# Rotary cross-attention values by Strassen's seven products, key weights loaded and split in every step

## The chip, the cores and the metric

The kernel runs on one NeuronCore of a Trainium2 chip. The metric is the device time of one execution in microseconds (us). Below, PE is the matrix engine, PEld its weight loads, DVE the vector engine, ACT the scalar engine, POOL the GpSimd engine and SP the queue that issues transfers.

## The reference

A two-layer Perceiver block works on 2 x 128 latent tokens of width 512 against a context of 2 x 2048 rows of width 512: cross-attention with rotary keys, self-attention, a sign-weight layer, a second cross-attention, a second self-attention, a mixture of experts. The change lies in the first of these alone:

```python
lat = layer_norm(latents, ln_lat_g, ln_lat_b)
ctx = layer_norm(context, ln_ctx_g, ln_ctx_b)     # 2 x 2048 x 512
q = lat @ Wq                                      # 16 heads of 64
k, v = jnp.split(ctx @ Wkv, 2, axis=-1)           # 1024 columns each
k = apply_rope(k, cos, sin)
attn = softmax(clip(q k^T * scale, -11, 11))
out = (attn @ v) @ Wo + bo
```

The products `ctx @ Wkv` (4096 x 512 x 2048) are made in three passes, high times high, high times low, low times high, with each operand split into a rounded part and a rest, so that the rounded form of the matmul keeps its accuracy.

## The kernel before

The context goes through `cross_attention_rotary` in `NC` = 8 blocks `n` of 512 rows, and each block in four steps `t` = 4n to 4n+3, one for each group of four heads: 32 steps in all. I call 4n, 4n+1, 4n+2, 4n+3 the first to fourth step of block n. Every engine runs a stream of its own, written out by hand, in order; semaphores join them. There is no scheduler.

- PE: in the first and third step `values(v)` makes half of the value columns of the block: four tiles of 128 rows x 512 columns, each 4 depths x 3 passes = 12 matmuls of 512 columns, 48 in a call and 96 in a block, into the four banks of `u_ps`. Behind it `transposes` turns two of the four depths of block n+1 into `u_ps`. Then in each step `project(t)` (24 matmuls into the two banks of `k_ps`), `scores(t-1)` (into all of `u_ps`) and `weigh(t-2)` (into `o_ps`).
- ACT: copies the values out of `u_ps` (`values`), writes the scaled context twice, as it is and rounded (`context`, into `ctx_full` and `ctx_hi`), takes exponents (`exponent`), and takes the square root for the layer norm two blocks ahead (`root`) in the third step.
- DVE: `turn(t)` rotates the keys, four multiplies out of `k_ps` and two of SBUF alone; `clip(t-1)`; and the layer norm of block n+2 in three pieces in the second, third and fourth step (`stats`, `spread`, `center`).
- POOL: `split` makes the context's low part from `ctx_full` and `ctx_hi`, two depths in every other step; `add_up(t-1)` adds the probabilities into the denominators, four instructions a step.
- SP: all weights are loaded and split once. `load_ctx` and `load_tab` have two buffers each.

The split of the weights is done before step 0, or at step 1 for two of the four key groups (`high_v`, `low_v`, `high_k`, `low_k`). PE's order in a step reads, cut:

```python
if t < NT and t % 2 == 0:
    values(v)
    ...
if t < NT:
    project(t)
if 1 <= t <= NT:
    scores(t - 1)
if t >= 2:
    weigh(t - 2)
```

## Time and profile before

| | us |
|---|---|
| median of three runs | 1193.29 (1192.87 to 1197.12) |
| the profiled execution | 1196.15 |
| its span, first to last instruction | 1194.4 |
| PE busy in it | 1174.4 |
| DVE, ACT, POOL busy | 688.8, 540.1, 217.0 |
| the stage of the change | about 0 to 542 of the span |

Times are of one execution on the slowest core. In a timeline a row is a run of equal instructions: start, time until the last of them ends, and how many. Matmul ends are modelled and overlap the next start, so a matmul's price is the distance between starts.

### The profile page before, as it was taken

How to read it: one execution, taken by the hardware profiler on the slowest of the kernel's cores; microseconds unless marked ns; L12 is line 12 of the kernel's file. 1: busy time of each engine (PE TensorE's matmuls, PEld its weight loads, DVE VectorE, ACT ScalarE, POOL GpSimd, SP SyncE). 2: the span in 40 equal slices, each digit the busy share in tenths (PEclk: the TensorE clock that was granted, in tenths of full speed). 3: DMA queues.
4: the chain of work that ended last, by engine and by line, in shares of the span. 5: the costliest groups of instructions: out<-in, count | busy, mean ns of one | idle time of the engine just before them, and what ended most of it. 6: DMA issues, size and time to landing. Idle time of an engine off the chain costs nothing.

```text
span 1194.4 us, 23415 instructions
## 1 busy us (share of the span) xinstructions
PE 1174.4 (98%) x9888; PEld 963.8 (81%) x9888; DVE 688.8 (58%) x1220; ACT 540.1 (45%) x907; POOL 217.0 (18%) x178
## 2 busy tenths in 40 slices
PE   8999999999999999999899999999999999999998
PEld 6888888888788888864546667888899999999997
DVE  4654554545464533466788885265765566566562
ACT  4433324332433322224359997373644544444441
POOL 2243343444333443350000000010000000000000
PEclk9999999999999999999989999999999999999999
DMA  8210201010100020245232324301545445445440
GB/s 302 71 55 1 66 2 52 4 36 19 36 19 2 27 72 1 83 139 212 96 152 79 136 108 178 142 1 72 228 159 211 161 192 211 157 195 207 158 162 19
DMA packets 28160, 126.06 MB, mean 106 GB/s; under 512 B 2715, under 2 KB 2971, under 8 KB 17572
## 3 DMA queue, kind: packets, MB, share of 16 engines
q1 hardware_dynamic: 28068, 124.74, 27.9%
q8 instruction: 69, 1.13, 0.4%
q14 instruction: 23, 0.19, 0.0%
HBM read 124.20 MB, written 0.52 MB: 104 GB/s over the span
## 4 chain that ended last, share of the span: by engine, by line
PE 49%; issue 2%; DVE 2%; ACT 2%; DVEq 0%
PE mid_bk L57 11%; PE mid_bk L58 10%; PE mid_bk L59 10%; PE mid_bk L1105 5%; PE mid_bk L1120 2%; PE mid_bk L1150 2%; PE mid_bk L1076 2%; PE mid_bk L995 2%; PE mid_bk L1140 1%; PE mid_bk L1249 0%; ACT sa_sc L1415 0%; PE mid_bk L1201 0%; PE mid_bk L1190 0%; PE mid_bk L1050 0%; PE mid_bk L986 0%
## 5 line engine op out<-in xcount | busy, mean ns | idle before, releaser
L565 POOL TENSOR_TENSOR norm_both<-norm_both,prob 128x512 f32<-128x512 f32 x118 | 155.4, 1317 | 145.6 <-DVE prob L357 138.2
L494 ACT ACTIVATE prob<-u_ps 128x512 f32<-128x512 f32 x128 | 66.2, 605 | 181.5 <-PE u_ps L667 181.5
L57 PE MATMUL mid_bk<-mo_x_hi,mo_w_hi 128*128 128x256 f32 x496 | 141.0, 284 | 0.0
L58 PE MATMUL mid_bk<-mo_x_lo,mo_w_hi 128*128 128x256 f32 x496 | 141.0, 284 | 0.0
L59 PE MATMUL mid_bk<-mo_x_hi,mo_w_lo 128*128 128x256 f32 x496 | 141.0, 284 | 0.0
L340 DVE TENSOR_TENSOR turned<-k_ps,tabs 128x512 f32<-128x512 f32 x32 | 22.1, 690 | 189.7 <-PE k_ps L59 189.6
L1788 DVE TENSOR_TENSOR mo_w_lo<-w_raw,mo_w_hi 128x2048 fp32r<-128x2048 f32 x32 | 73.3, 2292 | 72.7 <-ACT mo_w_hi L1497 72.7
L57 PE MATMUL k_ps<-ctx_hi,wk_hi 128*128 128x512 f32 x256 | 102.8, 402 | 0.0
L57 PE MATMUL u_ps<-wv_hi,ctx_hi 128*128 128x512 f32 x256 | 101.7, 397 | 0.8 <-ACT prob L494 0.8
L483 ACT ACTIVATE vals<-u_ps 128x512 f32<-128x512 f32 x64 | 38.3, 598 | 141.2 <-PE u_ps L59 141.1
L1497 ACT ACTIVATE mo_w_hi<-w_raw 128x2048 fp32r<-128x2048 f32 x32 | 61.2, 1913 | 87.9 <-PE mid_bk L59 87.9
L57 PE MATMUL mid_bk<-mo_w_hi,mo_h_hi 128*128 128x512 f32 x256 | 100.2, 391 | 0.0
L58 PE MATMUL k_ps<-ctx_lo,wk_hi 128*128 128x512 f32 x256 | 100.2, 391 | 0.0
L58 PE MATMUL u_ps<-wv_lo,ctx_hi 128*128 128x512 f32 x256 | 100.1, 391 | 0.0
L58 PE MATMUL mid_bk<-mo_w_lo,mo_h_hi 128*128 128x512 f32 x256 | 100.0, 391 | 0.0
L59 PE MATMUL u_ps<-wv_hi,ctx_lo 128*128 128x512 f32 x256 | 99.7, 389 | 0.0
L59 PE MATMUL k_ps<-ctx_hi,wk_lo 128*128 128x512 f32 x256 | 99.7, 389 | 0.0
L59 PE MATMUL mid_bk<-mo_w_hi,mo_h_lo 128*128 128x512 f32 x256 | 99.6, 389 | 0.0
L58 PEld LDWEIGHTS mid_bk<-mo_x_lo,mo_w_hi 128*128 128x128 f32 x496 | 95.9, 193 | 1.2
L57 PEld LDWEIGHTS mid_bk<-mo_x_hi,mo_w_hi 128*128 128x128 f32 x496 | 95.8, 193 | 1.2
L59 PEld LDWEIGHTS mid_bk<-mo_x_hi,mo_w_lo 128*128 128x128 f32 x496 | 95.8, 193 | 0.0
L1505 ACT ACTIVATE mo_hid<-mid_bk,mo_b_cur 128x256 f32<-128x256 f32 x128 | 53.7, 472 | 86.8 <-PE mid_bk L59 86.7
(264 smaller groups left out, 2357.2 us busy)
## 6 DMA issues: line engine op xcount, KB each, us to landing
w_raw<-in_w SPq DMA_DIRECT2D x64, 1024.0 KB, 6.3
ctx_raw<-in_ctx_rows SPq DMA_DIRECT2D x8, 1024.0 KB, 5.5
x_k<-in_ctx_T SPq DMA_DIRECT2D x8, 1024.0 KB, 7.0
x_val<-in_ctx_heads SPq DMA_DIRECT2D x8, 1024.0 KB, 5.0
tabs<-in_rot_tabs SPq DMA_DIRECT2D x8, 512.0 KB, 3.8
vals<-in_wq_rows SPq DMA_DIRECT2D x4, 512.0 KB, 7.6
ctx_raw<-in_wo SPq DMA_DIRECT2D x1, 2048.0 KB, 9.7
x_mask<-in_mask SPq DMA_DIRECT2D x2, 1024.0 KB, 9.0
```

The costliest lines, as they stand in the source:

```text
L57: pe.matmul(out, w_hi, x_hi, start=start, stop=False)
L58: pe.matmul(out, w_hi, x_lo, start=False, stop=False)
L59: return pe.matmul(out, w_lo, x_hi, start=False, stop=stop)
L483: act.activation(vals[:, i, hv * 512:(hv + 1) * 512], u_ps[:, i, :], ACT.Copy).then_inc(s["v_out"], 1)
L494: act.activation(prob[:, t % 2, i, :], u_ps[:, i, :], ACT.Exp).then_inc(s["exped"], 1)
L565: ins = pool.tensor_tensor(to, to, src, ALU.add)
L995: ins = pe.matmul(bk[b][:, m, :], normed_T[:, k, b * P:(b + 1) * P], (wq, wk, wv)[m][:, k, :], start=(m == 2 and k == 0), stop=(k == KD - 1))
L1076: pe.matmul(s_ps[:, a, :], normed_T[rows, g, b * P:(b + 1) * P], k_raw[rows, n % 2, c * 512:(c + 1) * 512], start=True, stop=True).then_in ...
L1105: ins = pe.transpose(turned_at(q, a)[:, k * P:(k + 1) * P], x_sc[:, n % 2, a, (4 * c + k) * P:(4 * c + k + 1) * P], ident[:])
L1497: act.activation(w2_hi[:, r, :, :], w2_raw[:, r, :, :], ACT.Copy).then_inc(mo["w2_hi"], 1)
L1505: act.activation(hid[:, r, n, :], h_ps[:, 2 * r + n // 2, (n % 2) * TOK:(n % 2 + 1) * TOK], ACT.Gelu_apprx_tanh, bias=b1_cur[:, r, n:n + 1 ...
L1788: dve.tensor_tensor(w2_lo[:, r, :, :], w2_raw[:, r, :, :], w2_hi[:, r, :, :], ALU.subtract).then_inc(mo["w2_lo"], 1)
```

## The change

Each block's values are a product of a 512 x 512 context block A with the 512 x 1024 weights B. A is cut into row halves and depth halves, B into depth halves and column halves; the product of the 2 x 2 blocks is made with seven products of half depth instead of eight, by the Winograd form of Strassen's scheme. Four sums of context blocks (S1 to S4) and four of weight blocks (T1 to T4) are needed, and each sum needs its own high and low part. For a row quarter pair `ip` (0 or 1) `values(n, ip)` makes seven `product`s of 2 depths x 3 passes = 6 matmuls of 512 columns, 42 a call, 84 a block. Three of them accumulate on a bank that already holds another product.

What is new, by engine:

- PE: `values(n, 0)` stands at the end of the second step, `values(n, 1)` between the two halves of `project` in the third. All four `transposes` of block n+1 stand at the head of the fourth step.
- DVE: `weight_sums` and seven `low_v` at the start; in every step `low_k(t+1)` ahead of the rotation; `sums(n)` in the first step (four half-tile sums in place in `ctx_full`), then `stats` and `spread` for block n+1 in that same step; `low_s(n)` in the second; `add_products` (five adds out of `u_ps`) at the end of the second and inside the third; `center` of block n+1 at the head of the third.
- ACT: `high_k(t+1)` in every step; `high_s(n)` and `root(n+1)` at the end of the first step; `keep_products` (two copies); `context` for all four depths at the head of the fourth.
- POOL: `split` for all four depths in the fourth step, ahead of `add_up`.
- SP: key weights (512 KB) are loaded in every step once the step before the last is projected; `ctx_raw` and `tabs` have one buffer each; the output weights are loaded behind the last value product.

Core of the diff:

```diff
+        a_of = {"A11": (0, 0, 0), "A12": (0, 1, 0), "A22": (0, 1, 1),
+                "S2": (1, 0, 0), "S4": (1, 1, 0), "S3": (1, 0, 1), "S1": (1, 1, 1)}
+        w_of = {"B11": 0, "B21": 1, "B22": 2, "T3": 3, "T1": 4, "T2": 5, "T4": 6}
...
             def load_tab(n):
-                if n >= 2:
-                    sp.wait_ge(s["rope"], 24 * (n - 1))
+                if n >= 1:
+                    sp.wait_ge(s["rope"], 24 * n)
...
+            def load_wk(t):
+                g = t % 4
+                if t >= 2:
+                    sp.wait_ge(s["k_mm"], 2 * (t - 1))
+                sp.dma_start(wk_raw[:, t % 2, :, :], I["wk_rows"][g * P:(g + 1) * P, :]
+                             .rearrange("p (k n) -> p k n", k=KD)).then_inc(s_wk[t % 2], 16)
...
+            for t in range(1, NT):
+                n, r = t // 4, t % 4
+                if t + 1 < NT:
+                    load_wk(t + 1)
+                if r == 0:
+                    load_tab(n)
+                if r == 3 and n + 2 < NC:
+                    load_ctx(n + 2)
...
+            def weight_sums():
+                dve.wait_ge(s["wv_in"], 64)
+                for n, (dst, a, b) in enumerate((("T1", "T3", "B11"), ("T2", "B22", "T1"), ("T3", "B22", "T3"),
+                                                 ("T4", "B21", "T2"))):
+                    dst, a, b = (wv_raw[:, w_of[m], :, :] for m in (dst, a, b))
+                    if n:
+                        dve.wait_ge(s["part_sum"], n)
+                    dve.tensor_tensor(dst, a, b, ALU.subtract).then_inc(s["part_sum"], 1)
+
+            def low_v(j):
+                dve.wait_ge(s["part_hi"], j + 1)
+                dve.tensor_tensor(wv_lo[:, j, :, :], wv_raw[:, j, :, :], wv_hi[:, j, :, :],
+                                  ALU.subtract).then_inc(s["part_lo"], 1)
...
+            def low_k(t):
+                dve.wait_ge(s["wk_hi"], t + 1)
+                dve.tensor_tensor(wk_lo[:, t % 2, :, :], wk_raw[:, t % 2, :, :], wk_hi[:, t % 2, :, :],
+                                  ALU.subtract).then_inc(s["wk_lo"], 1)
...
+            def sums(n):
+
+                dve.wait_ge(s["csplit"], 4 * n + 4)
+                for m, (dst, a, b, op) in enumerate((("A22", "A21", "A22", ALU.add), ("A21", "A11", "A21", ALU.subtract),
+                                                     ("A11", "A22", "A11", ALU.subtract),
+                                                     ("A12", "A12", "A11", ALU.subtract))):
+                    if m:
+                        dve.wait_ge(s["part_sum"], 4 + 4 * n + m)
+                    dve.tensor_tensor(full[dst], full[a], full[b], op).then_inc(s["part_sum"], 1)
+
+            def low_s(n):
+                for u in range(2):
+                    dve.wait_ge(s["part_hi"], NWB + 2 * n + u + 1)
+                    ks = slice(2 * u, 2 * u + 2)
+                    dve.tensor_tensor(s_lo[:, ks, :], ctx_full[:, ks, :], s_hi[:, ks, :],
+                                      ALU.subtract).then_inc(s["part_lo"], 1)
+
+            def add_products(n, ip):
+
+                v = 2 * n + ip
+                c11, c12 = vals[:, ip, 0:512], vals[:, ip, 512:1024]
+                c21, c22 = vals[:, 2 + ip, 0:512], vals[:, 2 + ip, 512:1024]
+                dve.wait_ge(s["v_kept"], 2 * v + 1)
+                dve.wait_ge(s["v_mm"], NWB * v + 2)
+                dve.tensor_tensor(c12, u_ps[:, 1, :], c11, ALU.add).then_inc(s["v_sum"], 1)
+                dve.wait_ge(s["v_mm"], NWB * v + 3)
+                dve.wait_ge(s["v_sum"], 5 * v + 1)
+                dve.tensor_tensor(c22, u_ps[:, 2, :], c12, ALU.add).then_inc(s["v_sum"], 1)
+                dve.wait_ge(s["v_mm"], NWB * v + 4)
+                dve.wait_ge(s["v_sum"], 5 * v + 2)
+                dve.tensor_tensor(c22, u_ps[:, 3, :], c22, ALU.add).then_inc(s["v_sum"], 1)
+                dve.wait_ge(s["v_mm"], NWB * v + 6)
+                dve.tensor_tensor(c21, u_ps[:, 2, :], c12, ALU.add).then_inc(s["v_sum"], 1)
+                dve.wait_ge(s["v_mm"], NWB * v + 7)
+                dve.tensor_tensor(c12, u_ps[:, 3, :], c12, ALU.add).then_inc(s["v_sum"], 1)
+
...
             for t in range(NT + 1):
-                n, g = t // 4, t % 4
+                n, r = t // 4, t % 4
+                if t < NT and r == 2 and n + 1 < NC:
+                    center(dve, n + 1)
+                if t + 1 < NT:
+                    low_k(t + 1)
                 if t < NT:
-                    turn(t)
+                    if r == 1:
+                        low_s(n)
+                    turn_first(t)
+                    if r == 2:
+                        add_products(n, 1)
+                    turn_second(t)
+                    if t == 0:
+                        for j in range(3, NWB):
+                            low_v(j)
+                    if r == 0:
+                        sums(n)
                 if t >= 1:
                     clip(t - 1)
-                if t == 1:
-                    low_k(2)
-                    low_k(3)
-                if t < NT and 2 <= n + 2 < NC:
-                    if g == 1:
-                        stats(dve, n + 2)
-                    elif g == 2:
-                        spread(dve, n + 2)
-                    elif g == 3:
-                        center(dve, n + 2)
-                if t == 28:
+                if t < NT:
+                    if r == 1:
+                        add_products(n, 0)
+                    if r == 0 and n + 1 < NC:
+                        stats(dve, n + 1)
+                        spread(dve, n + 1)
+                if t == 11:
                     dve.wait_ge(s["bo_in"], 16)
...
+            def high_k(t):
+                act.wait_ge(s_wk[t % 2], 16 * (t // 2 + 1))
+                if t >= 2:
+                    act.wait_ge(s["k_mm"], 2 * (t - 1))
+                act.activation(wk_hi[:, t % 2, :, :], wk_raw[:, t % 2, :, :], ACT.Copy).then_inc(s["wk_hi"], 1)
+
+            def high_s(n):
+                act.wait_ge(s["part_sum"], 4 + 4 * n + 4)
+                for u in range(2):
+                    ks = slice(2 * u, 2 * u + 2)
+                    act.activation(s_hi[:, ks, :], ctx_full[:, ks, :], ACT.Copy).then_inc(s["part_hi"], 1)
...
+            def keep_products(n, ip):
+
+                v = 2 * n + ip
+                c11 = vals[:, ip, 0:512]
+                act.wait_ge(s["v_mm"], NWB * v + 1)
+                if n >= 1:
+                    act.wait_ge(s["weighed"], 4 * n)
+                act.activation(c11, u_ps[:, 0, :], ACT.Copy).then_inc(s["v_kept"], 1)
+                act.wait_ge(s["v_sum"], 5 * v + 1)
+                act.wait_ge(s["v_mm"], NWB * v + 5)
+                act.activation(c11, u_ps[:, 0, :], ACT.Copy).then_inc(s["v_kept"], 1)
...
+                n, r = t // 4, t % 4
+                if t < NT and r == 3 and n + 1 < NC:
+                    for k in range(KD):
+                        context(n + 1, k, k)
+                if t + 1 < NT:
+                    high_k(t + 1)
+                if t == 0:
+                    for j in range(3, NWB):
+                        high_v(j)
...
+                if t < NT and r == 2:
+                    keep_products(n, 1)
                 if t >= 1:
                     exponent(t - 1)
-                if t < NT and n + 2 < NC and g == 2:
-                    root(act, n + 2)
+                if t < NT and r == 0:
+                    high_s(n)
+                    if n + 1 < NC:
+                        root(act, n + 1)
+                if t < NT and r == 1:
+                    keep_products(n, 0)
...
-                if t < NT and t % 2 == 0 and n + 1 < NC:
-                    for kk in range(2):
-                        split(n + 1, 2 * (t % 4 // 2) + kk)
+                if t < NT and t % 4 == 3 and n + 1 < NC:
+                    for k in range(KD):
+                        split(n + 1, k)
...
+            def values(n, ip):
+
+                v = 2 * n + ip
+                if n == 0 and ip == 0:
+                    pe.wait_ge(s["part_lo"], NWB)
+                if ip == 1:
+                    pe.wait_ge(s["v_sum"], 5 * v)
+                    pe.wait_ge(s["v_kept"], 2 * v)
+                for bank, (a, w) in enumerate((("A11", "B11"), ("S2", "T2"), ("S3", "T3"), ("S1", "T1"))):
+                    if ip == 0:
+                        pe.wait_ge(s["exped"], 16 * n + bank + 1)
+                    if bank == 1:
+                        pe.wait_ge(s["part_lo"], NWB + 2 * n + 2)
+                    if v == 9 and bank >= 2:
+                        pe.wait_ge(s["den_out"], bank - 1)
+                    product(n, ip, a, w, bank, True, True)
+                pe.wait_ge(s["v_kept"], 2 * v + 1)
+                product(n, ip, "A12", "B21", 0, False, True)
+                pe.wait_ge(s["v_sum"], 5 * v + 2)
+                product(n, ip, "A22", "T4", 2, False, True)
+                pe.wait_ge(s["v_sum"], 5 * v + 3)
+                product(n, ip, "S4", "B22", 3, False, True)
+
...
-                if t < NT and t % 2 == 0:
-                    v = t // 2
-                    if v == 0:
-                        pe.wait_ge(s["cfull"], KD)
-                    values(v)
-                    if v // 2 + 1 < NC:
-                        for kk in range(2):
-                            pe.wait_ge(s["v_out"], 4 * v + kk + 1)
-                            transposes(v // 2 + 1, 2 * (v % 2) + kk, kk)
+                n, r = t // 4, t % 4
+                if t < NT:
+                    if r == 3 and n + 1 < NC:
+                        for k in range(KD):
+                            transposes(n + 1, k, k)
+                    project(t, 0)
...
-                if t < NT:
-                    project(t)
-                if 1 <= t <= NT:
+                    if r == 2:
+                        values(n, 1)
+                    project(t, 1)
+                if t >= 1:
                     scores(t - 1)
                 if t >= 2:
                     weigh(t - 2)
+                if t < NT and r == 1:
+                    values(n, 0)
...
```

DVE around the first step of a block. In the kernel before, the stretch from the clip of a first step's probabilities on; `prob` holds probabilities, `cst` the layer norm's statistics, `turned` and `part` the rotated keys:

```order
L357 TENSOR_SCALAR prob<-prob 128x512 x4
L296 BN_STATS cst<-ctx_raw 128x6 x4
L340 TENSOR_TENSOR turned<-k_ps,tabs 128x512
L341 TENSOR_TENSOR turned<-k_ps,tabs 128x512
L345 TENSOR_TENSOR part<-k_ps,tabs 128x512
L346 TENSOR_TENSOR part<-k_ps,tabs 128x512
```

Behind a clip and the statistics the next rotation follows at once. In the changed kernel, from `sums` of a block's first step to the rotation of its second:

```order
L349 TENSOR_TENSOR ctx_full<-ctx_full 128x2x256 x4
L407 TENSOR_SCALAR prob<-prob 128x512 x4
L299 BN_STATS cst<-ctx_raw 128x6 x4
L304 BN_AGGR cmv<-cst 128x2 x4
L306 TENSOR_SCALAR cva<-cmv 128x4
L338 TENSOR_TENSOR wk_lo<-wk_raw,wk_hi 128x1024
L355 TENSOR_TENSOR s_lo<-ctx_full,s_hi 128x1024 x2
L386 TENSOR_TENSOR turned<-k_ps,tabs 128x512
L387 TENSOR_TENSOR turned<-k_ps,tabs 128x512
L395 TENSOR_TENSOR part<-k_ps,tabs 128x512
L396 TENSOR_TENSOR part<-k_ps,tabs 128x512
```

The context sums, the whole of the statistics, the key split and the sums' low parts now stand between one rotation and the next.

ACT at the same place, with the semaphores that each waits for. Before, the root stands behind exponents in the third step:

```order
L315 ACT_TABLE_LOAD
L315 ACTIVATE csd<-cva 128x4 [waits x0_c_var]
L494 ACT_TABLE_LOAD [waits x0_summed,x0_weighed]
L494 ACTIVATE prob<-u_ps 128x512 [waits x0_score]
L494 ACTIVATE prob<-u_ps 128x512 [waits x0_summed,x0_weighed,x0_score] x3
L483 ACTIVATE vals<-u_ps 128x512 [waits x0_weighed,x0_v_mm] x4
```

Changed:

```order
L519 ACTIVATE s_hi<-ctx_full 128x1024 [waits x0_part_sum]
L519 ACTIVATE s_hi<-ctx_full 128x1024
L318 ACT_TABLE_LOAD
L318 ACTIVATE csd<-cva 128x4 [waits x0_c_var]
L513 ACTIVATE wk_hi<-wk_raw 128x1024 [waits x0_k_mm,x0_wk_in0]
L557 ACT_TABLE_LOAD [waits x0_summed,x0_weighed]
L557 ACTIVATE prob<-u_ps 128x512 [waits x0_score]
L557 ACTIVATE prob<-u_ps 128x512 [waits x0_summed,x0_weighed,x0_score] x3
L546 ACTIVATE vals<-u_ps 128x512 [waits x0_weighed,x0_v_mm]
```

The rounded key weights of the next step (`wk_hi`) now stand behind the root, and the root behind DVE's `cva`.

POOL in a fourth step, changed (`ctx_lo` is the context's low part, `norm_both` the denominators):

```order
L631 TENSOR_TENSOR norm_both<-norm_both,prob 128x512 [waits x0_summed,x0_clipped]
L631 TENSOR_TENSOR norm_both<-norm_both,prob 128x512 [waits x0_summed] x3
L617 TENSOR_TENSOR ctx_lo<-ctx_full,ctx_hi 128x512 [waits x0_cfull] x4
L631 TENSOR_TENSOR norm_both<-norm_both,prob 128x512 [waits x0_summed,x0_clipped]
L631 TENSOR_TENSOR norm_both<-norm_both,prob 128x512 [waits x0_summed] x3
```

Before, two of the four `ctx_lo` rows stood there and two two steps earlier.

## Rows read from the trace of the kernel before

**Rows 1.** The page: busy time of each engine, granted clock in 40 slices

```profile
PE 1174.4 (98%) x9888; PEld 963.8 (81%) x9888; DVE 688.8 (58%) x1220; ACT 540.1 (45%) x907; POOL 217.0 (18%) x178
...
PEclk9999999999999999999989999999999999999999
```

**Rows 2.** Waits of PE, span 60 to 520 us, then 0 to 60

```profile
PE u_ps L667 <- ACT prob L494: 0.3, 1, 0.3
...
PE u_ps L57 <- ACT prob L494: 0.8, 1, 0.8
```

**Rows 3.** Timeline of PE, one step with values: start us, us, engine line op

```profile
114.94 0.50 PE L57 MATMUL u_ps<-wv_hi,ctx_hi 128*128 128x512 f32 x1
...
126.00 1.03 PE L602 MATMUL u_ps<-ident,ctx_raw 128*128 128x128 f32 x8
126.79 0.48 PE L57 MATMUL k_ps<-ctx_hi,wk_hi 128*128 128x512 f32 x1
...
132.42 2.07 PE L667 MATMUL u_ps<-q_T,turned 32*128 32x128 f32 x64
134.41 1.97 PE L683 MATMUL o_ps<-prob,vals 128*64 128x128 f32 x32
```

**Rows 4.** Timeline of DVE, steps around the same place

```profile
115.57 2.46 DVE L296 BATCH_NORM_STATS2 cst<-ctx_raw 128x6 f32<-128x512 f32 x4
...
132.53 0.69 DVE L345 TENSOR_TENSOR part<-k_ps,tabs 128x512 f32<-128x512 f32 x1 [1.36 <-PE k_ps L59]
...
134.33 0.68 DVE L351 TENSOR_TENSOR turned<-turned,part 128x512 f32<-128x512 f32 x1
135.13 1.90 DVE L357 TENSOR_SCALAR prob<-prob 128x512 f32<-128x512 f32 x4
136.94 0.37 DVE L301 BATCH_NORM_AGGREGATE cmv<-cst 128x2 f32<-128x6 f32 x4
137.35 1.08 DVE L303 TENSOR_SCALAR cva<-cmv 128x4 f32<-128x4 f32 x1
```

**Rows 5.** Timeline of ACT, the same steps

```profile
126.69 0.78 ACT L468 ACTIVATE ctx_full<-u_ps,vecs 128x512 f32<-128x512 f32 x1
127.35 0.78 ACT L468 ACTIVATE ctx_hi<-u_ps,vecs 128x512 fp32r<-128x512 f32 x1
...
134.50 2.07 ACT L494 ACTIVATE prob<-u_ps 128x512 f32<-128x512 f32 x4 [5.03 <-PE u_ps L667]
...
138.46 0.21 ACT L315 ACTIVATE csd<-cva 128x4 f32<-128x4 f32 x1 [0.59 <-DVE cva L303]
138.68 1.28 ACT L494 ACT_TABLE_LOAD   x1
```

**Rows 6.** Timeline of POOL, the same steps

```profile
128.21 2.63 POOL L551 TENSOR_TENSOR ctx_lo<-ctx_full,ctx_hi 128x512 fp32r<-128x512 f32 x2 [7.06 <-ACT ctx_hi L468]
137.11 5.40 POOL L565 TENSOR_TENSOR norm_both<-norm_both,prob 128x512 f32<-128x512 f32 x4 [6.26 <-DVE prob L357]
```

**Rows 7.** DVE and POOL at once: two timelines, and DVE's line 409 (min/median/max ns)

```profile
146.75 5.84 DVE L310 TENSOR_SCALAR ctx_raw<-ctx_raw,cmv,crs 128x512 f32<-128x512 f32 x4
...
L409 DVE TENSOR_TENSOR resid<-resid,bo x2: 684/1235/1786, 478.9 to 479.5; 128x512 f32<-128x512 f32 x2
...
479.02 6.09 POOL L565 TENSOR_TENSOR norm_both<-norm_both,prob 128x512 f32<-128x512 f32 x4 [15.07 <-DVE prob L357]
```

**Rows 8.** Timeline of the start, all engines

```profile
17.12 10.53 PE L614 MATMUL k_ps<-norm_both,vals 128*128 128x256 f32 x48
...
22.11 2.01 ACT L451 ACTIVATE wv_hi<-prob 128x1024 fp32r<-128x1024 f32 x2
...
27.30 0.58 PE L57 MATMUL u_ps<-wv_hi,ctx_hi 128*128 128x512 f32 x1
...
27.68 0.60 ACT L474 ACTIVATE q_T<-k_ps 128x512 f32<-128x512 f32 x1 [2.85 <-PE k_ps L614]
...
29.79 1.23 DVE L328 TENSOR_TENSOR wk_lo<-prob,wk_hi 128x1024 fp32r<-128x1024 f32 x1 [1.22 <-ACT wk_hi L456]
```

**Rows 9.** Transfers: KB each, median us from issue to landing

```profile
tabs<-in_rot_tabs SPq DMA_DIRECT2D x8, 512.0 KB, 3.8
```

**Rows 10.** Stretches behind a gap of PE: busy of each engine, granted clock

```profile
580.00:582.00 2.00, 0.66 (x4) 0.42 (x4) 1.89 (x7) 1.47 (x4) 0.00 (x0) 1.00 0.00 0
...
584.00:586.00 2.00, 2.00 (x23) 1.38 (x16) 0.93 (x2) 0.00 (x0) 0.00 (x0) 0.50 0.00 0
```

More of the change, by code:

```diff
@@ L185, in cross_attention_rotary @@
-        slabs = sb_in(st, "slabs", [P, 64 * 256 + (env["floor"] - env["base"]) // 4])
+        NWB = 7
+        wv_raw = place("wv_raw", [P, NWB, 2, 512], 0)
+        wv_lo, wv_hi = (place(n, [P, NWB, 2, 512], kb, F32R) for n, kb in (("wv_lo", 0), ("wv_hi", 28)))
+        wk_raw = place("wk_raw", [P, 2, KD, 256], 56)
+        wk_lo, wk_hi = (place(n, [P, 2, KD, 256], kb, F32R) for n, kb in (("wk_lo", 56), ("wk_hi", 64)))
+        ctx_full = place("ctx_full", [P, KD, 512], 72)
+        s_lo, s_hi = (place(n, [P, KD, 512], kb, F32R) for n, kb in (("s_lo", 72), ("s_hi", 80)))
@@ L633, in project, with product @@
[L633 to L646 removed]
+            def product(n, ip, a, w, bank, start, stop):
+                src, kh, th = a_of[a]
+                rows = slice(256 * th + ip * P, 256 * th + ip * P + P)
+                for kk in range(2):
+                    k = 2 * kh + kk
+                    hi, lo = ((ctx_hi[:, n % 2, k, rows], ctx_lo[:, n % 2, k, rows]),
+                              (s_hi[:, k, rows], s_lo[:, k, rows]))[src]
+                    for part_a, part_b in ((hi, wv_hi), (hi, wv_lo), (lo, wv_hi)):
+                        ins = pe.matmul(u_ps[:, bank, :], part_a, part_b[:, w_of[w], kk, :],
+                                        start=(start and kk == 0 and part_a is hi and part_b is wv_hi),
+                                        stop=(stop and kk == 1 and part_a is lo), skip_group_check=True)
+                ins.then_inc(s["v_mm"], 1)
```

270 lines of the change are left out of this document (102 added, 168 removed).

## The prediction

> **What bounds the kernel now.** I read the page first: PE is busy for 1174.4 of 1194.4 us, at full clock nearly throughout, and no other engine above 58% [rows 1]. Busy PE is not PE at its peak, so I went to PE's waits: between 60 and 520 us it waits 0.3 us in all, before that 0.8 us once for an exponent [rows 2]. The stage of the change is therefore PE's own time, and each matmul taken out there is worth its distance between starts, as long as nobody else gets late. DVE, at half load on average, is the engine to watch: the change gives it work in a fixed order, and PE's new waits hang on the end of that order.
>
> **What is removed.** The 48 matmuls of a value call take from 114.94 to 126.00 [rows 3]: 0.230 us each. A call of 42 takes 9.7 us. Eight blocks with 12 fewer each: 96 x 0.230 = **22.1 us less**. Everything else that PE does stays: `project` 5.7 (126.79 to 132.42), `scores` 2.0, `weigh` 1.9, eight transposes 0.8 [rows 3].
>
> **What is added, and its prices.** Per block DVE gets four key splits and two sum splits of 1024 columns (1.2 each, as the 1.23 of wk_lo [rows 8]), four context sums and ten product adds (0.68 each alone, 0.60 in a queue [rows 4]), some 17 us in all. ACT gets four key copies and two sum copies of 1.0 (2.01 for two [rows 8]) for eight copies of values less. On average that fits. Whether it hides is a question of order, at three places.
>
> *1. From the rotation of the first step to the value products of the second, every block.* Zero is the start of `scores` in the first step (132.42 in the trace). PE then has scores 2.0, weigh 1.9, project 5.7, scores 2.0, weigh 1.9, values 9.7: it would be through at 23.2. But the last two products wait for `add_products`, and DVE reaches it only after: end of the rotation, 2.6 (rows 132.42 to 134.33 + 0.68 [rows 3, 4]); four sums that each wait for the one before, 2.8; clip 1.8 and statistics 2.5, aggregate and cva 0.4 + 1.1 [rows 4]; then, over on ACT, the root 0.3 and the key copy 1.0, which stands behind it [rows 5, 8]; back on DVE the key split 1.2, the sum splits 2.4, six rotation instructions 3.6, clip 1.8, two product adds 1.4; and on PE the last two products, 2.8. Sum: 25.7. PE ends **2.5 us late**, part of it ahead of the first product (the exponents stand on ACT behind the same root, key copy and a 1.28 table load [rows 5]), part ahead of the sixth.
>
> *2. The first projection of a new block.* It waits for all four `split` on POOL, now queued behind `add_up`. Zero is the end of scores in the third step. POOL starts on add_up at 2.7 (exponents 2.1, last clip 0.5), needs 5.4 for it and 5.3 for the splits (2.63 for two) [rows 4 to 6]: 13.4. PE has weigh 1.9, transposes 1.6, project 5.7, scores 2.0, weigh 1.9: 13.1. Late by **0.3**. ACT is in time: its eight context writes at 0.66 [rows 5] end at 8.0, the key copy at 9.1.
>
> *3. DVE and POOL at once.* Line 409, an add of two SBUF tiles, takes 0.684 us alone and 1.786 with an add_up begun beside it, and that add_up takes 6.09 in place of 5.40; four scalings of the clips' kind and size, which take 1.90 for four alone [rows 4], take 5.84 beside an add_up [rows 6, 7]. So one waits for the other's running instruction. The multiplies out of `k_ps` show no such rows. The Trainium skill, "SBUF — State Buffer", section "Who interferes with whom", calls this pair of ports an exclusive lock for a whole instruction, for DVE instructions with two SBUF inputs and those that use both ports. That speaks against this change: by it the sum is the forecast's, by a collision only where one has been seen it would be the first rival's. The change adds just such instructions. In the fourth step the key split (1.1) and one of the two SBUF adds of the rotation (0.6) fall between the four splits: these end 1.8 later, the stall of place 2 is 0.3 + 1.8 = **2.1**, in two blocks 1.4, because there the first instruction of add_up is a short copy. The clip and add_up behind shift too, and the next key split pushes add_up out by 1.2 more, to some 4 us behind the next zero of place 1, so that the rotation's two SBUF adds of the first step wait for it: 1.9 more there, **4.4** in all. In the last block, without statistics and root, the same collisions leave 1.9.
>
> *4. The start.* Before, value products begin at 27.30, with weights split while PE makes the queries [rows 8]. Now the first key copy stands behind the last query copy (27.68 + 0.5), so: key copy to 29.2, key split to 30.4, project 30.5 to 36.2. DVE has four dependent weight sums at 1.25 (to 35.4), three weight splits (38.9), the second key split (40.1), then the first rotation, for which `project(1)` waits: 41.4 to 47.1; scores to 49.2. DVE: rotation ends 43.7, four weight splits 48.4, context sums 51.2, statistics and cva 54.3. ACT: root 54.5, key copy 55.5, table load 56.8, first exponent 57.4. Only now is a bank of `u_ps` free for the values; DVE's key split 56.7, sum splits 59.1, rotation 62.7, clip 64.5, two adds 65.9, and the last products end at 68.7. PE's own work in it is 5.7 + 5.7 + 2.0 + 9.7 = 23.1, from 27.3 to 50.4. Late by 18.3; less the 0.8 that before waits [rows 2]: **17.5**.
>
> Costed at nothing: key loads (512 KB; a table of that size lands in 3.8 [rows 9], from the end of a projection to its next use are 13 us, cover of 5 on top of load, copy and split); the single table buffer (its load starts with the end of the fourth step's rotation and lands about as the next block's second half is projected; late by 1 at most, behind POOL's delay); the single context buffer (loaded a step and a half ahead); the late output weights (20 us of PE lie between). The output bias at step 11 and the reciprocals and scaling at 18 and 19 stand in a fuller DVE queue: 2 in all.
>
> **The sum.** -22.1 + 17.5 + 6 x 4.4 (blocks 1 to 6) + 1.9 + 5 x 2.1 + 2 x 1.4 + 2 = **+39.0 us**. From the profiled execution, 1196.15, that is 1235.2; it lies 2.9 above the median of the runs, so in their terms **1232**.
>
> **The rivals.**
> - *The lock costs little*: POOL's or DVE's collisions fall between instructions. For it: most overlaps in before left no mark on rotation rows. Against: line 409 and the scalings. Then -22.1 + 17.5 + 6 x 2.5 + 7 x 0.3 + 1 = +13.6: **1207**.
> - *The order has room after all* (the other side): if the DVE chain of place 1 is shorter than 23.2 rather than 25.7, for instance because dependent sums and adds follow as closely as independent ones (0.6, some 1 us less) and cva doesn't meet an add_up (0.9 less), and the lock costs nothing, only the start is left: -22.1 + 17.5 = -4.6, **1189**, no change that can be told. It decides from 2.5 us less in the chain. It turns faster only if the start also costs under 16.
> - *The clock falls too.* Behind gaps of PE around 580 us the granted clock went from 1.00 to 0.50, 2.4 to 1.2 GHz [rows 10]; what PE does in 4 us of it takes 2 more. The new gaps are 2 to 3 us at 13 places, and 5 and 8 at the start. Ahead of the sixth product it hides behind DVE; at a block's first projection it moves the next zero but gives POOL the same time. I take 1 each: **1247**. The skill's page "TensorE: Matmul & The Clock Gate", Part 1, says that idleness is what throttles the array; the rows at 580 agree, and by it the range must reach up.
>
> **How the numbers follow.** Forecast 0.55 (its own range 1221 to 1240), lock costs little 0.23, clock or worse 0.12, room after all 0.10. Cutting 0.10 at each end gives 1203 to 1246. This kernel's measurement can't tell less than about 0.5%, 6 us, from no change. Faster 0.04, same 0.07, slower 0.89.
>
> **What would show it.** Right: value matmuls 672 in place of 768; PE waits of 2 us for POOL's `ctx_lo` at each block's first projection; waits ahead of the first and sixth product of each second step for ACT's exponents and DVE's adds; PE idle near 36 to 41 and 49 to 57 us; cva, key split and rotation SBUF adds with long maxima; some 66 us a block where before has 62. Wrong: blocks of 62 with no lock marks (first rival), or 59 (second); waits for `wk_raw` or `tabs` transfers, which I took as hidden; a clock under 1.00 within the blocks.

## The result, and the profile after

The changed kernel takes **1218.92 us** (median of 4 runs, 1216.31 to 1220.99) against 1193.08 for the kernel before on the same chip: ratio **1.0209**, interval 1.0177 to 1.0242. It is 25.8 us slower; I had forecast 39.0 slower (1232, range 1203 to 1246). The profiled execution has a span of 1219.2.

The page answers [rows 1]: PE has 96 matmuls fewer and is busy for 11.7 us less, over a span that is 24.8 longer. PEclk, the granted clock in tenths, shows a 7 in the second slice.

```profile
PE 1162.7 (95%) x9792; PEld 948.5 (78%) x9792; DVE 810.3 (66%) x1383; ACT 566.8 (46%) x922; POOL 230.9 (19%) x178
...
PEclk9799999999999999999989999999999999999999
```

What PE waits for, 14 to 75 us and then 75 to 520 us (us in total, times, longest), where [rows 2] has 0.8 and 0.3:

```profile
PE u_ps L694 <- ACT prob L557: 6.6, 1, 6.6
PE k_ps L57 <- DVE turned L387: 3.4, 1, 3.4
PE k_ps L57 <- DVE wk_lo L338: 2.9, 1, 2.9
...
PE u_ps L694 <- ACT prob L557: 9.0, 6, 2.1
PE k_ps L57 <- issue: 7.5, 7, 1.4
PE u_ps L694 <- DVE vals L368: 3.7, 7, 0.6
PE u_ps L694 <- DVE s_lo L355: 1.0, 1, 1.0
```

By the places of the prediction, the first three are the start (place 4). Of the others, the second line is the first projection of a block (place 2; "issue" because the profile names no releaser), the rest the value products of the second step (place 1).

PE's timeline at the start, and in one block around a first projection, the two `scores` behind it and the value call:

```profile
30.44 0.53 PE L57 MATMUL k_ps<-ctx_hi,wk_hi 128*128 128x512 f32 x1 [2.89 <-DVE wk_lo L338]
...
41.18 0.77 PE L57 MATMUL k_ps<-ctx_hi,wk_hi 128*128 128x512 f32 x1 [3.43 <-DVE turned L387]
...
48.34 2.07 PE L757 MATMUL u_ps<-q_T,turned 32*128 32x128 f32 x64
56.98 0.77 PE L694 MATMUL u_ps<-wv_hi,ctx_hi 128*128 128x512 f32 x1 [6.57 <-ACT prob L557]
...
161.77 0.47 PE L57 MATMUL k_ps<-ctx_hi,wk_hi 128*128 128x512 f32 x1 [1.41 <-issue]
...
167.42 2.07 PE L757 MATMUL u_ps<-q_T,turned 32*128 32x128 f32 x64
...
182.45 0.50 PE L694 MATMUL u_ps<-wv_hi,ctx_hi 128*128 128x512 f32 x1 [1.47 <-ACT prob L557]
...
190.41 0.50 PE L694 MATMUL u_ps<-wv_hi,ctx_hi 128*128 128x512 f32 x1 [0.55 <-DVE vals L368]
```

The same stretch on DVE and POOL, to be held against [rows 4, 6]:

```profile
156.16 1.39 DVE L338 TENSOR_TENSOR wk_lo<-wk_raw,wk_hi 128x1024 fp32r<-128x1024 f32 x1 [6.41 <-ACT wk_hi L513]
...
168.74 1.74 DVE L398 TENSOR_TENSOR turned<-turned,part 128x512 f32<-128x512 f32 x1
170.40 0.68 DVE L401 TENSOR_TENSOR turned<-turned,part 128x512 f32<-128x512 f32 x1
...
178.03 1.27 DVE L306 TENSOR_SCALAR cva<-cmv 128x4 f32<-128x4 f32 x1
180.52 1.23 DVE L338 TENSOR_TENSOR wk_lo<-wk_raw,wk_hi 128x1024 fp32r<-128x1024 f32 x1 [1.22 <-ACT wk_hi L513]
```

```profile
155.16 6.50 POOL L617 TENSOR_TENSOR ctx_lo<-ctx_full,ctx_hi 128x512 fp32r<-128x512 f32 x4
163.63 6.29 POOL L631 TENSOR_TENSOR norm_both<-norm_both,prob 128x512 f32<-128x512 f32 x4 [1.97 <-DVE prob L407]
175.28 5.35 POOL L631 TENSOR_TENSOR norm_both<-norm_both,prob 128x512 f32<-128x512 f32 x4 [5.35 <-DVE prob L407]
```

The reader is to see an overlap in each long row: the rotation's sum at 168.74 takes 1.74, not 0.68, with an `add_up` running to 169.9; `cva`, four columns, takes 1.27 with another running; and the four splits take 6.50, not 5.3, with DVE's key split among them.

**A second number for what follows.** The first matmul of the self-attention behind the changed stage starts at 542.85 before and at 563.93 after. So 21.1 of the profile's 24.8 arise in the changed stage; 3.7 come later, from code that is the same in both. I call the first difference the **stage's**, and give it for each run (one execution each, with its sign against before).

### The profile page after: what moved, and what is told of

Read it like the earlier page. It is cut to its first block, busy times and chain, and to the rows that moved or that the text cites. A ratio compares the mean times of both kernels' runs of the same rounds, so it can differ in the third digit from the quotient of the medians.

```text
span 1219.2 us, 23526 instructions
## 1 busy us (share of the span) xinstructions
PE 1162.7 (95%) x9792; PEld 948.5 (78%) x9792; DVE 810.3 (66%) x1383; ACT 566.8 (46%) x922; POOL 230.9 (19%) x178
## 4 chain that ended last, share of the span: by engine, by line
PE 46%; DVE 3%; issue 2%; ACT 2%; DMA 0%; DVEq 0%; ACTq 0%
PE mid_bk L57 10%; PE mid_bk L58 10%; PE mid_bk L59 10%; PE mid_bk L1198 5%; PE mid_bk L1213 2%; PE mid_bk L1243 2%; PE mid_bk L1169 2%; PE mid_bk L1088 2%; PE mid_bk L1233 1%; DMA w_raw<-in_w 0%; PE mid_bk L1342 0%; DVE mo_w_lo L1875 0%; DVE mo_w_lo L1881 0%; ACT sa_sc L1508 0%; PE mid_bk L1294 0%
## 5 line engine op out<-in xcount | busy, mean ns | idle before, releaser
L631 POOL TENSOR_TENSOR norm_both<-norm_both,prob 128x512 f32<-128x512 f32 x118 | 159.1, 1348 | 208.5 <-DVE prob L407 201.1
L1881 DVE TENSOR_TENSOR mo_w_lo<-w_raw,mo_w_hi 128x2048 fp32r<-128x2048 f32 x32 | 73.3, 2291 | 74.5 <-ACT mo_w_hi L1590 74.5
L338 DVE TENSOR_TENSOR wk_lo<-wk_raw,wk_hi 128x1024 fp32r<-128x1024 f32 x32 | 43.5, 1359 | 63.7 <-ACT wk_hi L513 63.7
L1789 DVE CUSTOM_DVE_ANT_0 x_sc<-mid_bk,x_mask 128x512 f32<-128x512 f32 x128 | 80.9, 687 | 5.6 <-issue 5.6
L1198 PEld LDWEIGHTS mid_bk<-ident,x_sc 128*128 128x128 f32 x512 | 55.3, 140 | 25.8 <-ACT x_pT L1530 18.7
L1875 DVE TENSOR_TENSOR mo_w_lo<-w_raw,mo_w_hi 128x2048 fp32r<-128x2048 f32 x31 | 70.8, 2285 | 4.9 <-ACT mo_w_hi L1582 4.9
L1523 ACT ACTIVATE x_sc<-x_sc,x_negtop 128x1024 f32<-128x1024 f32 x64 | 73.5, 1149 | 1.2 <-DVE x_negtop L1796 1.2
## 6 DMA issues: line engine op xcount, KB each, us to landing
wv_raw<-in_wv_rows SPq DMA_DIRECT2D x4, 512.0 KB, 12.1
```

The lines of the kernel that those rows point to most:

```text
L631: ins = pool.tensor_tensor(to, to, src, ALU.add)
L1198: ins = pe.transpose(turned_at(q, a)[:, k * P:(k + 1) * P], x_sc[:, n % 2, a, (4 * c + k) * P:(4 * c + k + 1) * P], ident[:])
L1523: act.activation(cut, cut, ACT.Exp, bias=x_neg[:, n % 2, a:a + 1], accum_out=x_den[:, n % 2, half, a:a + 1]).then_inc(x["exped"], 1)
L1789: dve.tensor_tensor_reduce(x_sc[:, n % 2, a, cols], s_ps[:, a, :], mask[:, b, cols], 1.0, -3.0e38, ALU.add, ALU.max, x_tops[:, n % 2, a, c ...
L1875: dve.tensor_tensor(w1_lo[:, r, :, :], w1_raw[:, r, :, :], w1_hi[:, r, :, :], ALU.subtract).then_inc(mo["w1_lo"], 1)
L1881: dve.tensor_tensor(w2_lo[:, r, :, :], w2_raw[:, r, :, :], w2_hi[:, r, :, :], ALU.subtract).then_inc(mo["w2_lo"], 1)
```

## The experiments

All are edits of the changed kernel. Medians against the kernel before on the same chip (1192.4 to 1193.4).

| run | median | ratio (interval) | stage's |
|---|---|---|---|
| changed kernel | 1218.9 | 1.0209 (1.0177 to 1.0242) | +21.1 |
| e1_root_behind | 1213.8 | 1.0166 (1.0136 to 1.0195) | +19.1 |
| e2_norm_later | 1216.7 | 1.0192 (1.0169 to 1.0215) | +15.4 |
| e3_splits_first | 1227.9 | 1.0295 (1.0267 to 1.0323) | +31.9 |
| e4_start_early | 1211.1 | 1.0148 (1.0115 to 1.0182) | +15.6 |
| e5_narrow | 1193.1 | 0.9994 (0.9982 to 1.0006) | -2.3 |
| e6_nokeys | 1191.8 | 0.9991 (0.9976 to 1.0005) | -3.0 |
| e7_start_mix | 1203.0 | 1.0074 (1.0047 to 1.0101) | +8.9 |
| e8_five | 1185.5 | 0.9955 (0.9932 to 0.9978) | -8.9 |
| e9_pool_waits | 1235.1 | 1.0337 (1.0309 to 1.0365) | +41.4 |
| e10_five_waits | 1189.4 | 0.9976 (0.9962 to 0.9990) | -5.6 |
| e11_four | 1187.6 | 0.9961 (0.9947 to 0.9975) | -7.9 |
| e12_one_shared | 1189.2 | 0.9971 (0.9952 to 0.9989) | -4.4 |

My theory at the outset: DVE's order and the lock with POOL cost the blocks their gain, and the order of copies and splits costs the start. The rivals: POOL's lateness without the lock, or the key loads.

**e1_root_behind.** ScalarE, first step:

```diff
+                        high_k(t + 2)
                         root(act, n + 1)
```

> ScalarE's copy of the next step's key weights moved ahead of the root in each first step; nothing else. If place 1 is set by VectorE's chain (it waits some 1.2 us for that copy between cva and the key split, and PE stands 2.0 us a block behind the chain): about 1.2 us in each of seven blocks, 8 us less, 1210, and the waits ahead of the second step's value products shrink. Rival, POOL's add_up and the lock set place 1: no change, 1219.

The median is 5.1 lower, but the stage gave only 2.0 of it. The wait of the first product for the exponents fell from 9.0 to 3.0, and one product later PE waited 6.0 for `s_lo`, the low parts of the context sums, instead of 1.0: the sum splits stand behind the key split. A wait removed ahead of an in-order queue moved one instruction on.

**e2_norm_later.** DVE's `stats` and `spread` of the next block, and the root, go from the first step to the third:

```diff
-                    if r == 0 and n + 1 < NC:
+                if t < NT and r == 2 and n + 1 < NC:
                     stats(dve, n + 1)
                     spread(dve, n + 1)
...
+                if then_center:
+                    center(dve, n + 1)
                 dve.wait_ge(s["v_mm"], NWB * v + 6)
```

> Statistics, aggregates, cva and the root of the next block moved out of the first step into the third (centring between the third and the fourth product add). By the theory of the chain it is 3.5 us shorter with the wait for the root and its table gone, against a stall of 2.0 a block: 7 x 2.0 = 14 less, and some 4 less at the start, where the first exponent stands behind the same root: about 1201. Rival, the third step has no room for them (VectorE's moved 5.4 us come back as a wait of the transposes or of the second rotation): 1215 to 1225. Rival, the lock sets place 1: 1215.

The median fell by 2.2, the stage's number by 5.7. The third step had room. But the shorter chain now meets POOL's `add_up`. DVE, and POOL's row beside it:

```profile
173.99 2.14 DVE L338 TENSOR_TENSOR wk_lo<-wk_raw,wk_hi 128x1024 fp32r<-128x1024 f32 x1 [1.68 <-ACT wk_hi L513]
176.05 4.53 DVE L355 TENSOR_TENSOR s_lo<-ctx_full,s_hi 128x1024 fp32r<-128x1024 f32 x2
```

```profile
172.39 7.10 POOL L631 TENSOR_TENSOR norm_both<-norm_both,prob 128x512 f32<-128x512 f32 x4 [5.36 <-DVE prob L409]
```

Key split and sum splits take 6.7 together where the changed kernel's take 3.6: 3.1 of the 3.5 us taken out of the chain went back into the lock.

**e3_splits_first.** POOL:

```diff
+                if t % 4 == 2 and n + 1 < NC:
+                    continue
                 if t < NT and t % 4 == 3 and n + 1 < NC:
                     for k in range(KD):
                         split(n + 1, k)
+                    add_up(t - 2)
```

> POOL makes the four context splits of the next block ahead of the add_up of the second step's probabilities instead of behind it. If PE's wait of 1.4 us at a block's first projection (place 2) is for POOL: 7 x 1.4 = 10 less, 1209. Rival, the two add_ups that now follow the splits reach into the next block and take VectorE's rotation and ScalarE's exponents with them: no change or up to 10 more.

9.0 slower, the rival's case. The wait at place 2 is gone, so it was POOL's; but PE's largest waits of 75 to 520 us became:

```profile
PE u_ps L697 <- ACT prob L557: 20.1, 6, 4.1
PE u_ps L697 <- DVE s_lo L355: 3.1, 1, 3.1
```

All waits of 75 to 520 us grew by only 3.2, from 21.2 to 24.4, while the stage grew by 10.8. The rest is TensorE's clock: in six blocks it is granted at 0.50 for a while, and some 55 matmuls start 0.43 us apart in place of 0.23, about 11 us. One such stretch (us, us, busy and number of PE, PEld, DVE, ACT, POOL, then the granted clock, DMA share, GB/s):

```profile
248.50:255.30 6.80, 5.91 (x14) 4.66 (x15) 6.80 (x12) 2.89 (x6) 0.00 (x0) 0.50 0.00 0
```

**e4_start_early.** On DVE `weight_sums()` first, then both key splits; on ScalarE:

```diff
             queries(1)
+            high_k(0)
+            high_k(1)
             queries(2)
-            queries(3)
-            high_k(0)
             for j in range(3):
                 high_v(j)
+            queries(3)
```

> Order at the start only: weight sums, then both key splits at once on VectorE; both key copies and three value copies between the query copies on ScalarE. If the start is lost to the order of the copies and splits (VectorE is idle from 14 to 29 us), project(0) begins at 28 in place of 30.4, the 3.4 us wait of project(1) goes, and the first value product comes at 50 in place of 57: 7 us less, 1212. Rival, the value weights' transfers land too late for the sums (issued up to 9.6 us, 12 us to land): half of it, 1215. Rival, TensorE's clock stays at its lower level longer, since the gaps move: 1217.

7.8 less, and PE's rows stand where they were expected:

```profile
28.50 0.49 PE L57 MATMUL k_ps<-ctx_hi,wk_hi 128*128 128x512 f32 x1 [1.27 <-DVE wk_lo L338]
...
50.32 0.77 PE L696 MATMUL u_ps<-wv_hi,ctx_hi 128*128 128x512 f32 x1 [8.30 <-ACT prob L558]
```

DVE's weight sums start at 22.22, when the last value weights have landed, instead of 30.30. So the order made this part of place 4. Not all of it: the first value product still waits 8.3 for the exponents.

**e5_narrow.** POOL's tiles cut:

```diff
-                        ins = pool.tensor_tensor(to, to, src, ALU.add)
+                        ins = pool.tensor_tensor(to[:, :, 0:16], to[:, :, 0:16], src[:, :, 0:16], ALU.add)
```

> POOL's add_up adds 16 of 128 columns (all but the first copy of a group): most of the sum of the denominators is left out, and with it nearly all of POOL's 5.4 us a step; PE, ScalarE and VectorE do the same work as in the changed kernel. If POOL delays place 2 (its splits stand behind add_up) and the lock stretches the rotation's sum of place 1: 7 x 1.4 = 10 and 7 x 1.1 = 8 less, 1201. Rival, POOL only delays place 2: 1209. Rival, POOL's time doesn't matter: 1219.

25.8 less, more than even the first theory's 18: the stage gave 23.4. At place 1 nothing but 0.2 a block is left:

```profile
PE u_ps L694 <- DVE vals L368: 1.1, 6, 0.2
```

In its DVE rows the rotation's sum takes 0.68 and `cva` 0.17. From the start of `scores`, the chain to the key split takes 10.9 where the changed kernel's takes 13.1 (167.42 to 180.52): 2.2 less, the two lock marks.

**e6_nokeys.**

```diff
             def low_k(t):
+                if t >= 2:
+                    return
                 dve.wait_ge(s["wk_hi"], t + 1)
```

(likewise the load and the copy.)

> Key weights are loaded and split in the first two steps alone; every later step uses the two pieces that are there (the keys of half of the heads are left out). This takes the key copy, the key split and the wait between them out of the chain of place 1 (2.4 us with 2.0 of stall) and one lock collision out of place 2 (0.1 of the splits' 6.5). By the theory of the chain: 7 x 2.0 = 14 less and 1 to 2 at the start, 1204. Rival, VectorE's place in the queue is made by POOL's lock: 1215. Rival, the loads themselves cost (queue, bandwidth): less than 1200.

27.2 less (stage 24.0), where 15 were expected. I had priced the meeting of key split and context splits at 0.1. POOL's splits show more:

```profile
150.72 5.43 POOL L623 TENSOR_TENSOR ctx_lo<-ctx_full,ctx_hi 128x512 fp32r<-128x512 f32 x4
```

5.43 in place of 6.50, and the wait at place 2 falls from 7.5 to 1.7. So of the 1.41 at a block's first projection 1.0 is one DVE instruction, the key split, locking POOL out. e5 and e6 take away different things and win nearly the same, 23.4 and 24.0: each alone brings DVE and POOL back under PE's time; the loss was an excess over a threshold, not a sum of shares.

**e7_start_mix.** e2 and e4 together, and:

```diff
-                if t < NT and r == 0:
+                if t < NT and r == 0 and n:
                     high_s(n)
+                if t == 1:
+                    high_s(0)
```

> The early start and the later statistics together, and in the first block alone the exponents ahead of the copies of the context sums. If the start is a chain of copies and splits: the first value product comes at 42 us in place of 50 (early start) and 57 (changed kernel), the second one waits until 47 for the split of the context sums, the last ends at 56: 5 to 7 us less than the early start alone, and 2 for the statistics: 1203. Rival, the gap between the first and the second product costs what is gained (and the clock falls there): 1209.

1203.0, as expected; the first product starts at 43.65, the second at 48.58 (42 and 47 forecast). The stage's 12.2 are e2's 5.7, e4's 5.5 and 1.0 that no run separates: the start and the blocks add up.

**e8_five.** e7, and:

```diff
-                if 0 < t < NT - 1:
+                if 0 < t < NT - 1 and r != 1:
                     low_k(t + 1)
...
                     turn_second(t)
+                if r == 1:
+                    low_k(t + 1)
```

with two of the four splits on DVE between its two halves of the rotation in the fourth step.

> e7_start_mix, with the key split of the second step behind the rotation instead of ahead of the split of the context sums, and with two of the four context splits of a block on VectorE. If VectorE's order and POOL's queue hold PE back: 7 x 1.0 (s_lo), 7 x 0.55 (product adds) and 7 x 1.4 (place 2) less than e7_start_mix: 1183, below the kernel before. Rival, the lock between VectorE and POOL turns the shared splits and the sum splits into longer ones (in e2_norm_later the same two took 4.53 instead of 2.35 beside an add_up): 1192 to 1197.

**1185.5**, 17.6 under e7 and 0.45% under the kernel before: the lowest median of all. PE's waits of 75 to 520 us:

```profile
PE u_ps L705 <- DVE vals L368: 4.0, 6, 1.4
PE k_ps L57 <- issue: 0.5, 2, 0.3
PE u_ps L768 <- ACT prob L565: 0.3, 1, 0.3
```

Some 3 us of the 17.8 that the stage gained over e7 are none of the edit's aims. Behind the wait for `s_lo` in the first block, 3.3 in both, the clock fell in the profiled execution of e7 and not in that of e8. The same stretch in e7, then in e8:

```profile
48.00:54.00 6.00, 5.42 (x13) 4.29 (x14) 5.97 (x12) 0.00 (x0) 0.57 (x1) 0.50 0.01 4
```

```profile
48.00:54.00 6.00, 5.69 (x24) 4.42 (x24) 6.00 (x12) 0.00 (x0) 0.00 (x0) 1.00 0.01 3
```

**e9_pool_waits.**

```diff
                 pool.wait_ge(s["clipped"], 4 * t + 4)
+                if g == 3 and t < NT - 1:
+                    pool.wait_ge(s["part_lo"], NWB + 2 * (n + 1) + 2)
```

> The changed kernel, all work kept; POOL's add_up of each fourth step waits until VectorE has made the context sums' splits of the next block. e5_narrow took away POOL's lateness and the lock together; this takes away one meeting of the lock at place 1 alone (cva takes 1.27 in place of 0.17 beside that add_up) and leaves place 2 as it is. If the lock makes the stall of place 1: cva at 0.17, 6 or 7 x 1.1 = 7 to 8 less, 1211. Rival, e5_narrow gained by POOL being free, not by the lock: the stall stays and the later add_up makes others wait, 1219 to 1228.

A miss: 16.2 slower in place of 7 to 8 faster. DVE, from `cva` to the clips, and POOL:

```profile
182.63 0.17 DVE L306 TENSOR_SCALAR cva<-cmv 128x4 f32<-128x4 f32 x1
...
189.83 1.03 DVE L398 TENSOR_TENSOR turned<-turned,part 128x512 f32<-128x512 f32 x1
190.79 1.78 DVE L401 TENSOR_TENSOR turned<-turned,part 128x512 f32<-128x512 f32 x1
192.50 2.51 DVE L407 TENSOR_SCALAR prob<-prob 128x512 f32<-128x512 f32 x4
```

```profile
187.65 6.07 POOL L633 TENSOR_TENSOR norm_both<-norm_both,prob 128x512 f32<-128x512 f32 x4 [13.12 <-issue]
```

The mechanism did what I said: `cva` takes 0.17 with POOL held back. But the same `add_up` now meets the rotation's two sums and the clips behind it (0.35, 1.1 and 1.1 longer than in the changed kernel), closer to the product adds, and the wait ahead of the sixth product grows from 3.7 to 17.7, up to 3.1 each. The waits for exponents fall from 9.0 to 3.8, so all waits of 75 to 520 us grow by 7.8, from 21.2 to 29.0. The stage grew by 20.3. Most of the other 12.5 is the clock: at each of the six long waits it goes to 0.50, and some 55 matmuls start 0.43 apart, about 11 us. The sixth product here, then the same place in the changed kernel:

```profile
196.45:199.20 2.75, 2.75 (x7) 2.17 (x8) 0.69 (x1) 0.73 (x1) 2.59 (x3) 0.50 0.00 0
```

```profile
190.40:193.20 2.80, 2.79 (x12) 2.33 (x13) 1.38 (x2) 1.10 (x2) 2.64 (x3) 1.00 0.00 0
```

Not a wrong mechanism but a wrong price: I had counted what the wait frees, and neither what it moves onto nor the clock behind longer waits.

**e11_four, e10_five_waits, e12_one_shared.** e11 is e8 with all four splits on POOL; e10 is e8 with e9's wait; e12 is e8 with one shared split:

```diff
-                        for k in (2, 3):
+                        for k in (3,):
```

> e8_five without the context splits shared with VectorE: the order of the second step alone beside e7_start_mix. If e8_five's 17.6 under e7_start_mix came from the order (s_lo 7.4, product adds 3.7) and from place 2 (7.5) as the waits say: 1193. Rival, the two are one stall moved about (what one place gives back the other takes): 1203 or 1186.

> e8_five with the wait of e9_pool_waits: the sum splits at 2.35 in place of 3.44 and the rotation's sum at 0.68 in place of 1.77 in the second step. If the 4.0 us of waits for the product adds left between 75 and 520 us come from the lock: 3 to 4 less, 1182. Rival, the shift moves the meeting to the rotation and the adds behind: no change, 1185.

> e11_four with one of the four context splits of a block on VectorE (e8_five has two). If what VectorE takes over comes back as waits for its product adds only above some amount: POOL is 1.3 earlier, the 7.5 us of waits at place 2 nearly gone, the product adds as in e11_four (none) or 1 to 2 in all: 1179 to 1181. Rival, the gain and the loss are proportional: half of the difference between e11_four and e8_five, 1186.

e11: 1187.6, where 1193 and a rival at 1186 stood; the rival fits. The order of the second step alone gives 15.4 of e8's 17.6, by the medians. PE waits 7.5 at place 2 and for no product add; in e8 it waits 0.5 and 4.0: shared splits carry the wait from one place to the other. e10: 1189.4, no gain; waits for the adds rise to 5.9. e12: 1189.2 against 1180 hoped for, with 1.1 at place 2 and 5.4 for the adds. So e8, e10, e11 and e12 lie within 4 us, and their order among each other isn't settled: their intervals overlap. The clock is most of what parts their stages. In the profiled executions some 8, 13 and 23 matmuls of e11, e10 and e12 start 0.43 apart in place of 0.23, and none of e8. With 0.2 us taken off for each, the stage's numbers are about -8.9 (e8), -9.5 (e11), -8.2 (e10) and -9.0 (e12). So sharing none, one or two of the splits can't be told apart here, nor can e10's wait.

## Why the prediction was right, and where it was off

The sign, the four places and their mechanisms stood in the trace as foretold: 9792 matmuls (96 fewer), PE late for exponents, product adds, POOL's splits and at the start. The size was too high: 1218.9 lies in the whole range but under the 1221 to 1240 given for the forecast itself, and a block behind the first takes 62.5 to 64.1, where some 66 were foretold. Without the 3.7 of the later stages the total would lie nearer to the first rival's 1207 than to 1232, so it is the traces that bear the forecast out, not the total. The sizes, from the waits:

- *Matmuls removed, -22.1:* the count is right, and so nearly is the price. In e5, with little but the start in the way, a block takes 59.6 where before's takes 61.95 (61.7 and 64.0 in one block): 2.4 less where 2.8 were forecast, with 0.2 a block of named waits.
- *Start, +17.5:* `project(1)` at 41.4 forecast, 41.18 measured; first exponent 57.4 and 56.24; first product behind it at 56.98; the last product ends at 68.75, where 68.7 was forecast. Right, but otherwise made up: 12.1 us of waits net of before's 0.8, and some 5 at the lower clock of 1.2 GHz (0.43 us a matmul, from 56.98 on among others), which the sum had left to a rival. The forecast had PE wait there for DVE's adds, which it never did. e5's stage, where little but this term is left, gives -2.3 + 22.1 = 19.8: 12.4 of waits at the start, some 4.5 of clock there, and 0.4 a block of gaps.
- *Place 1, 6 x 4.4 + 1.9 = 28.3:* **mis-sized**, and the largest error. Waits of 9.0 + 3.7 + 1.0 = 13.7, 2.0 a block. From the start of `scores` to the end of the last product 25.8 passed (167.42 to 193.2), where the chain and the lock made 27.6. Two inputs were off. The `add_up` ended 2.5 behind the start of `scores` (169.92), not 4, so the lock caught one of the rotation's two SBUF sums, not both (1.06 in place of 1.9); and a clip behind other DVE work takes 1.35 for four, not the 1.8 of [rows 4], where it followed the exponents (2 x 0.45 less).
- *Place 2, 5 x 2.1 + 2 x 1.4 = 13.3:* **mis-sized**, 7.5: five waits of 1.4 and two of 0.2. POOL started 2.7 behind the end of `scores` (147.13 to 149.82) and its splits 8.0, both as forecast. Only the key split (1.1) held them up. The rotation's second sum, which I had put among them too, waited for them instead: it began at 160.46, before they ended at 161.66, and took 1.75.
- *Extras, +2:* the waits name none of them; `tabs` held DVE for 0.80, and PE for nothing.
- *Later stages, 0:* 3.7 measured (below). By luck this offset part of the error: the stage's forecast was +39, its result +21.1.

The waits sum to 12.1 + 13.7 + 7.5 = 33.3. With the removed 22.1 that is 11.2; the stage shows 21.1. About 5 is the clock at the start (some 25 matmuls at 0.43). Some 5, 0.6 a block, no wait names. Most of them come with the waits: a wait is counted from the modelled end of the matmul before it, and the matmul behind it takes longer. At 189.47 and 190.41 two starts lie 0.94 apart, 0.71 more than the usual 0.23, and 0.55 of it is named; the next start follows 0.33 behind. That is an estimated 0.15 to 0.3 for each of 21 waits, some 4 in all; the rest stays open.

The rival "the lock costs little" is refuted, not by e5's total, since e5 makes POOL early too, but by its rows: with the `add_up` cut down the chain of place 1 is shorter by the two lock marks alone, 2.2, and the stalls are gone. (That rival's sum comes to +13.5, not 13.6, which changes nothing.) The rival "the order has room after all" had the right arithmetic: without lock marks the chain is 25.8 - 2.2 = 23.6 against PE's 23.2, and e5 and e6 come out at "only the start is left", 1192 to 1193, where I had put 1189. Its condition, no lock, is what didn't hold. "The clock falls too" held at the start and in the stage behind, not within the changed kernel's blocks: 1.00 there, with waits up to 2.1. It did within the blocks of e3 and e9, whose waits are longer.

The Trainium skill, "SBUF — State Buffer", section "Who interferes with whom", has VectorE and GpSimd hold their shared port exclusively for a whole instruction. e9 agrees: `cva` 1.27 beside POOL and 0.17 without, and the length moved on with the `add_up`. All DVE rows of the stage that were seen to grow were SBUF-to-SBUF instructions, by up to 1.1 each, near the 1.35 of one POOL add. In e5, with POOL's adds cut short, one key split grew by 0.3 and nothing else.

## What to carry to other kernels

Fewer TensorE operations help only as far as the engines that prepare them stay under TensorE's new, shorter time; work out that chain in its order, with the root, the table load and the copies that stand in it, before counting matmuls. The scheme does pay here, by 0.24 to 0.45% in four orders, once sum splits stand ahead of key splits, statistics in a later step and start-up sums ahead of the first projection. Holding an engine back to spare another a shared port moves the meeting; see first what is queued where it will land. And a wait that grows may cost the clock besides: in e3 and e9 that was more than the waits grew by.

## What the runs showed of the hardware

**The clock behind a wait.** In the changed kernel PE waits up to 2.1 us within the blocks, and the granted clock stays at 1.00 there. Six waits of 2.7 to 3.1 in e9 and six of 3.0 to 4.1 in e3 each came with a stretch at 0.50. In e4 it also fell once at a wait of 2.1, and in e8 it didn't at one of 3.3. So the wait's length alone doesn't decide it.

**The later stages.** Busy times and, third from the right, the granted clock in stretches of 10 us from 30 us behind the start of the self-attention, changed kernel:

```profile
593.93:603.93 10.00, 6.80 (x54) 4.04 (x44) 8.69 (x20) 8.15 (x36) 1.04 (x1) 1.00 0.00 1
603.93:613.93 10.00, 10.00 (x60) 6.01 (x62) 5.39 (x13) 1.40 (x3) 0.00 (x0) 0.83 0.07 10
613.93:623.93 10.00, 9.44 (x33) 3.77 (x26) 6.83 (x30) 0.80 (x2) 0.00 (x0) 0.70 1.00 402
```

and e1_root_behind, the same place in the program:

```profile
591.93:601.93 10.00, 6.78 (x53) 4.04 (x44) 8.67 (x20) 8.16 (x36) 1.04 (x1) 1.00 0.00 1
601.93:611.93 10.00, 9.34 (x64) 4.76 (x62) 6.10 (x15) 1.60 (x4) 0.00 (x0) 1.00 0.16 41
611.93:621.93 10.00, 9.81 (x37) 4.76 (x38) 9.62 (x41) 0.60 (x1) 0.00 (x0) 1.00 0.93 380
```

Same code, same gaps, and the clock falls in one and not in the other. From the self-attention's start to the end of the span it is 655.3 in the changed kernel and 654.9 in e2, and 650.4, 650.6 and 650.5 in e1, e5 and e7, where the clock stays full here. The kernel before, at 651.5, falls here as the changed kernel does (0.83 and 0.68), so this stretch explains e1 and not the 3.7. The changed kernel falls once more, 67.6 us behind the start of the self-attention, where before does not:

```profile
631.50:634.90 3.40, 3.40 (x10) 1.53 (x14) 2.10 (x11) 3.40 (x8) 0.00 (x0) 0.50 0.00 0
```

```profile
610.40:613.80 3.40, 3.40 (x15) 1.49 (x14) 3.01 (x16) 3.40 (x8) 0.00 (x0) 1.00 0.03 12
```

That is 1.0 of the 3.7, by the distance between the same matmuls in both. The other 2.7 arise 290 to 310 us behind the start, where the changed kernel's clock falls at 873.9 and before's at another place, at 832.0; no run here settles how much of the 2.7 is its doing.

So medians of this kernel carry up to 5 us that hang on where the clock falls, and e1's 5.1 is mostly that. One and the same program shows it too: e8 took 1184.3 to 1185.6 us in six executions, at a mean granted clock of 0.996 to 1.000, and 1190.3 to 1193.2 in four, at 0.989 to 0.991. What decides it no run here tells.
